# Expert work in jobs of 384 and 256 rows, the first of them among the pieces of the last batch's router

## The chip, the cores and the metric

The kernel runs on one core of one Trainium2 chip. The metric is the device time of one execution in microseconds (us). A core has five engines that run their own instruction lists in order and wait for each other on semaphores: PE (TensorE, matrix products and transposes), DVE (VectorE), ACT (ScalarE), POOL (GpSimd) and SP (SyncE, which here issues most of the DMAs).

## The reference

Two layers on a batch of 8 sequences of 512 tokens with 256 features, all in float32. Layer 0 is an attention, then a mixture of experts behind a router; layer 1 is a second attention and a product with quantized numbers. The part that the change touches is the mixture. Its input is `cat -> int_W1 -> silu -> int_W2 -> norm`, a row of 256 numbers for each token; each token goes to its two best experts, into a slot of a buffer that holds 80 rows for each expert and batch, and each expert is a two-layer perceptron on its 640 rows:

```
probs = softmax(x @ Wr + br);  topk_p, topk_e = top_k(probs, 2)      # x: (8, 512, 256), 8 experts
pos = position of the token among those of its batch that chose the expert
keep = pos < 80
flat_idx = (e_flat * B + b_idx) * 80 + min(pos, 79)
buf = zeros(8 * 8 * 80, 256).at[flat_idx].add(x_rep * keep)          # (expert, batch, slot)
h = relu(buf[e] @ W1[e] + b1[e])                                     # 640 x 256 @ 256 x 1024
y = h @ W2[e] + b2[e]                                                # 640 x 1024 @ 1024 x 256
out = sum over the two choices of y[flat_idx] * p * keep
```

So the 640 rows of an expert are ordered by batch: rows 0 to 399 are those of batches 0 to 4, and row 384 lies inside batch 4.

## The kernel before

**Layer 0 as a pipeline over the batches.** `iteration(b1, b2, b3)` does three things at once: the token part of batch b1 (`token_stream`), the attention of batch b2 (`unit`), and the router part of batch b3 (`router_stream`). The program runs iteration(0, -, -), (1, 0, -), a hardware loop over (b+1, b, b-1), then (-, 7, 6) and last (-, -, 7), in which the router of batch 7 is alone.

**The order is written by hand.** Each engine has its own version of each stream as a Python generator. A generator yields the slot at which its next piece is due; the dictionary `AT` holds these slots. `interleave` goes through the slots 0 to 63, puts one attention unit at every even slot, and `advance` then runs every stream's pieces that are due, one stream after the other in the order in which they were handed to `started`. What comes out is one fixed instruction list per engine. Negative slots run ahead of the first unit; without an attention unit they run when `interleave` comes to slot 0 on DVE (but for `var1`), and earlier, by explicit calls of `advance`, on PE and ACT.

**The router's chain, in its order.** On DVE: moments of x1 (var1), z (normed x1), h1 (nA times the gathered gain, L1183, which waits for the four gathers of `pw` rows), its sum (L1186), moments (var2), h2 (normed with the root that ACT takes in sd2), h2a and h2b (times and plus rows gathered from `cptm`), later y_in, var3, f1, f2, f3 (the last norm), r_in to `rows` (softmax of 8 logits, the two picks, positions, row numbers), which ends in `sidx` (L1271). On POOL: 4 gathers of `pw`, 4 of `cptm`, the products for the t source (L665, L667), 4 gathers of `ms`, the products for the s source (L676, L678), and at the end 8 scatters of nB's rows into `buf_d` (L715). On PE: four sources turned (L767: x, t, h, s; ACT copies them to `cat`, L1004), 16 products with `wint` (L775), 8 with `wint2` (L787), turns of f (L795), the router's 8 products (L803), and sums that give the positions (L811). A float32 product is recorded as two instructions. On SP: loads of `ids` and `boff`, the store of x1 (L612), the load of xN where there is a b2 (L615), the store of the gates (L618).

**The expert stage.** After the last iteration, behind a barrier and with buffers of its own, `expert_loop` does expert after expert, 640 rows each. SP loads rows, b1, W1 (L1432), W2 and b2 (L1434) of expert k when expert k-2 is through, two sets of buffers, and stores y of expert k-2 (L1421). PE turns the 5 row tiles (L1451), multiplies them by W1 (L1463, two halves of 320 columns for each of 8 groups of hidden units, into four banks of PSUM in turn), turns the next expert's rows, and multiplies by W2 (L1475, 5 tiles of 128 rows, 8 products each). ACT takes the ReLU out of PSUM (L1488) into `hid`, of which there is one buffer; DVE copies the turned rows (L1497, L1498) and adds b2 (L1512).

**Layer 1** (`layer1`) comes behind the expert stage and a barrier; it gathers y rows from `y_d`. It is not touched.

## Time and profile before

| | us |
|---|---|
| timed runs | 2714.54, 2724.48, 2725.84 (median 2724.48) |
| profiled execution | 2714.43, of which 2712.4 are the span |
| set-up and the iterations before (-, 7, 6), to 1523.9 | 1523.9 |
| iteration (-, 7, 6), to 1698.5 | 174.6 |
| last iteration (router of batch 7), to 1796.6 | 98.1 |
| expert stage, to 2105.0 | 308.4 |
| layer 1, to 2712.4 | 607.4 |

Over the span PE was busy 78%, DVE 54%, ACT 38% and POOL 31%, and the mean clock granted to TensorE was 0.843 of full speed. All data moved by DMA came to 128.54 MB, 47 GB/s over the span.

In the rows below times are us from the start of the span. A timeline row has start, duration, engine, line and operation, what it writes and reads, the shape, the count where equal neighbours are merged, and in brackets how long the engine was idle before it and what ended that. "PE" rows are products, "PEld" rows weight loads, which overlap them; "SPq" rows are SP's issues of DMAs. The clock is a share of 2.4 GHz.

### The profile page before, as it was taken

The page shows a single profiled execution, that of the slowest core. Times are in us where ns is not written, and L with a number is a line of the kernel's source. Part 1 is how long each engine was busy: PE and PEld are TensorE (multiplying, and loading weights), DVE is VectorE, ACT ScalarE, POOL GpSimd, SP SyncE. Part 2 cuts the span into 40 slices and gives each one's busy share as a digit, 9 for nine tenths or more (in the row PEclk, how much of TensorE's full clock was granted, in tenths as well). Part 3 has the DMA queues.
Part 4 walks back from the last instruction along what each step waited for, and adds up shares of the span by engine and source line. Part 5 has one row for each costly group of instructions (what it writes and reads, how often), then busy time and mean ns, then how long its engine had stood idle before and what let it go on. Part 6 is the DMA issues. An engine that isn't in the chain of part 4 may idle for free. (4 is left out here: it accounts for less than half of the span.)

```text
span 2712.4 us, 33502 instructions
## 1 busy us (share of the span) xinstructions
PE 2108.4 (78%) x11774; PEld 1338.9 (49%) x11774; DVE 1455.8 (54%) x3626; ACT 1024.5 (38%) x2535; POOL 854.1 (31%) x585
## 2 busy tenths in 40 slices
PE   6437879779778878878778798349999496969697
PEld 5215545445444444545445455237777254535454
DVE  2357687577587587577678545220110245464635
ACT  2015545345445345355345355112222241515142
POOL 0253345245354354354254311310000332232311
PEclk9568979779878878878878888669999787979889
DMA  6100020120110200200200200222221301020200
GB/s 239 41 18 1 1 88 1 34 71 1 46 58 1 76 29 1 81 24 1 81 24 1 71 24 15 72 101 105 101 78 44 111 25 56 12 68 0 80 0 16
DMA packets 62592, 128.54 MB, mean 47 GB/s; under 512 B 14564, under 2 KB 39258, under 8 KB 60130
## 3 DMA queue, kind: packets, MB, share of 16 engines
q1 hardware_dynamic: 46570, 76.19, 8.1%
q0 software_dynamic: 15872, 50.35, 6.3%
q8 instruction: 95, 1.56, 0.2%
q14 instruction: 55, 0.45, 0.1%
HBM read 97.04 MB, written 29.46 MB: 47 GB/s over the span
## 5 line engine op out<-in xcount | busy, mean ns | idle before, releaser
L1039 ACT ACTIVATE att_buf<-att_buf,nmin 128x384 f32<-128x384 f32 (+3 forms) x512 | 287.4, 561 | 500.5 <-DVE nmin L1355 500.2
L879 PE MATMUL bank<-kk,qT 32*128 32x512 f32 (+2 forms) x1024 | 321.3, 651 | 86.1 <-DVE nmin L1355 85.4
L706 POOL TENSOR_TENSOR big<-ex_at,kx 128x2048 f32<-128x2048 f32 x64 | 236.0, 3711 | 202.9 <-DVE xt_na L1149 131.9
L906 PE MATMUL bank<-ident,att_buf 128*128 128x128 f32 x1280 | 230.2, 317 | 15.9 <-ACT att_buf L1047 15.0
L652 POOL TENSOR_TENSOR big<-kx 128x1280 f32<-128x1280 f32 x64 | 163.3, 2570 | 211.7 <-ACT kx L978 149.3
L920 PE MATMUL bank<-att_buf,vp 128*32 128x128 f32 x2560 | 218.6, 308 | 0.0
L1047 ACT COPY att_buf<-bank 128x384 f32<-128x384 f32 (+3 forms) x512 | 208.6, 408 | 17.9 <-PE bank L920 16.8
L1344 DVE TENSOR_TENSOR att_buf<-bank,wdiag 128x128 f32<-128x128 f32 x384 | 92.9, 283 | 181.8 <-PE bank L884 180.5
L879 PEld LDWEIGHTS bank<-kk,qT 32*128 32x128 f32 x1024 | 109.4, 213 | 160.0 <-DVE nmin L1355 108.3
L906 PEld LDWEIGHTS bank<-ident,att_buf 128*128 128x128 f32 x1280 | 170.3, 165 | 27.2 <-ACT att_buf L1039 21.7
L715 POOL DMA_INDIRECT buf_d<-nB,sidx x64 | 62.6, 977 | 323.4 <-DVE sidx L1271 306.3
L920 PEld LDWEIGHTS bank<-att_buf,vp 128*32 128x32 f32 x2560 | 135.7, 121 | 56.9 <-issue 46.9
L1488 ACT ACTIVATE hid<-bank,eb 128x320 f32<-128x320 f32 x128 | 67.5, 527 | 240.2 <-PE bank L1463 240.2
L1149 DVE TENSOR_REDUCE xt_na<-big 128x64 f32<-128x1024 f32 x128 | 151.8, 1209 | 11.0 <-POOL big L706 10.2
L1705 POOL TENSOR_SCALAR kf<-kf 128x512 f32<-128x512 f32 x40 | 67.4, 1684 | 256.1 <-ACT kf L1870 255.2
L1463 PE MATMUL bank<-eb,ew 128*128 128x320 f32 x512 | 141.3, 437 | 1.7 <-DVE eb L1498 1.7
L1475 PE MATMUL bank<-ew,hid 128*128 128x256 f32 x640 | 139.6, 379 | 0.6 <-ACT hid L1488 0.6
L1355 DVE CUSTOM_DVE_ANT_0 att_buf<-bank,att_buf 128x128 f32<-128x128 f32 (+3 forms) x320 | 137.5, 444 | 0.0
L1475 PEld LDWEIGHTS bank<-ew,hid 128*128 128x128 f32 x640 | 121.0, 190 | 17.2 <-ACT hid L1488 1.1
L775 PE MATMUL bank<-cat,wint 128*128 128x512 f32 x256 | 123.3, 618 | 0.7 <-ACT cat L1004 0.7
L1463 PEld LDWEIGHTS bank<-eb,ew 128*128 128x128 f32 x512 | 98.4, 192 | 42.6 <-DVE eb L1498 2.1
L824 PE MATMUL bank<-wvl,cT 128*128 128x448 f32 (+1 forms) x256 | 76.3, 464 | 49.0 <-issue 40.6
(342 smaller groups left out, 3970.1 us busy)
## 6 DMA issues: line engine op xcount, KB each, us to landing
ew<-in_eW SPq DMA_DIRECT2D x16, 1024.0 KB, 8.0
buf_d<-zero SPq DMA_DIRECT2D x8, 640.0 KB, 7.8
er<-buf_d SPq DMA_DIRECT2D x8, 640.0 KB, 4.3
y_d<-yy SPq DMA_DIRECT2D x8, 640.0 KB, 9.2
xt_na<-in_xT SPq DMA_DIRECT2D x8, 512.0 KB, 3.5
nA<-in_xN SPq DMA_DIRECT2D x8, 512.0 KB, 3.5
x_d<-x SPq DMA_DIRECT2D x8, 512.0 KB, 3.6
kf<-x_d SPq DMA_DIRECT2D x8, 512.0 KB, 3.2
```

The source lines that it names most:

```text
L652: pool.tensor_tensor(prod[:, lo:hi], spread(kx[:, t, 0:D], 1, hi - lo), spread(kx[:, t, DH * lo:DH * lo + D], 1, hi - lo, DH), ALU.mult)\
L706: pool.tensor_tensor(pv[:, c * P:(c + 1) * P, :].rearrange("p (h d) o -> p o h d", d=DH), spread(ex[:, t, :, 8 * c:8 * c + 8], 3, DH), spr ...
L775: mm = pe.matmul(bank[SIDE[o]][:], wint[:, order[n], o * P:(o + 1) * P], cat[:, n, :], start=(n == 0), stop=(n == 7))
L879: pe.matmul(bank[u % 2][:, 0:n], qT[r:r + 32, g, i * P:(i + 1) * P], kk[r:r + 32, g, T * i * P:T * i * P + n], start=True, stop=False)
L906: mm = pe.transpose(bank[3 + u % 2][:, j * P:(j + 1) * P], pr[:, u % NPR, j * P:(j + 1) * P], ident[:])
L920: mm = pe.matmul(bank[5][r:r + 32, i * P:(i + 1) * P], vp[:, j, p, DH * c:DH * c + 2 * DH], prT[:, (u + x) % 3, j * P:(j + 1) * P], start= ...
L1039: act.activation(pr[:, u % NPR, 0:n], pr[:, u % NPR, 0:n], ACT.Exp, scale=-1.0, bias=nmin[:, u % 4:u % 4 + 1], accum_out=rsum[:, i, h:h + ...
L1047: act.copy(prT[:, u % 3, 0:n], bank[3 + u % 2][:, 0:n]).then_inc(s("prT_ok"), 1)
L1149: dve.tensor_reduce(nA1[:, t, c * w:(c + 1) * w], pv[:, c * w:(c + 1) * w, :], X, ALU.add).then_inc(s("pv_used"), 1)
L1355: dve.tensor_tensor_reduce(dst if x else tiled(dst), lg[:, 0:n] if x else tiled(lg[:, 0:n]), add, 1.0, LARGE, ALU.add, ALU.min, nmin[:, (u ...
L1463: mm = pe.matmul(bank[n % 4][:, 0:W], ew1[:, k % 2, m, o * P:(o + 1) * P], eb[:, k % 2, m, c * W:(c + 1) * W], start=(m == 0), stop=(m == ...
L1475: mm = pe.matmul(bank[4 + n % 4][:, 0:D], hid[:, m, t * P:(t + 1) * P], ew2[:, k % 2, m, :], start=(m == 0), stop=(m == KH - 1))
```

## The change

- The stage `expert_loop` and its buffers go. The work of an expert is cut into two jobs, one of its rows 0 to 383 and one of its rows 384 to 639: first the eight jobs of 384 rows, for all experts, then the eight of 256 rows. Each expert's weights are so loaded twice.
- The jobs run inside the last iteration, iteration(-, -, 7), as a third stream (`expert_stream`) on PE, ACT and DVE behind `router_stream`, with slots of its own. Jobs 0, 1 and 2 have theirs among the router's slots; from job 3 on (on PE from the W2 products of job 2 on) they follow the router's last pieces.
- Buffers lie in layer 0's own: one set in `big` and `ex_at`, one in `kk` and `att_buf`, the hidden units and y in `kk`. Products with W1 use two banks of PSUM instead of four, those with W2 two instead of four.
- Job 0's rows and weights are loaded in the iteration before, (-, 7, 6), once its `ss_ok` has come, ahead of xN. Those of job k from 2 on are issued when job k-2's W2 products are done. SP waits for `e_sent`, which POOL sets when the scatters of batch 7 have landed, ahead of job 8's loads (the first of 256 rows).
- PE turns the rows of job k+1 between the W1 and W2 products of job k, ahead of the wait for job k's last ReLU (before it was behind that wait).

The slots, as `yield` in the streams have them:

```
PE : -4 turned(0) first(0) turned(1) | 2 second(0) | 10 first(1) turned(2) | 28 second(1; tile 0)
     33 second(1; 1, 2) first(2; 0, 1) | 43 first(2; 2) | 47 first(2; 3..7) turned(3) | 55 second(2), job 3, 4, ...
ACT: -4 relu(0) | 11 relu(1) | 38 relu(2; 0, 1) | 43 relu(2; 2) | 50 relu(2; 3..7), job 3, ...
DVE: -4 rows_in(0) | 7 rows_in(1) | 10 rows_out(0) | 12 rows_in(2) | 30, 40, 43 rows_out(1; 0, 1, 2)
     53 rows_in(3) | 62 rows_out(2), rows_in(4), rows_out(3), ...
```

The core of the diff:

```diff
+                JOBS = [(e, lo, hi) for lo, hi in ((0, 3), (3, ST)) for e in range(E)]
+                JT = [hi - lo for _, lo, hi in JOBS]
+                tiles_upto = lambda k: sum(JT[0:k])
...
+                                    for k in range(1, len(JOBS)):
+                                        n = k % 2
+                                        if k >= 2:
+
+                                            sp.wait_ge(s("e_y_mm"), tiles_upto(k - 1))
+                                        if k == E:
+                                            sp.wait_ge(s("e_sent"), 1)
+                                        for dst, src in expert_first(*JOBS[k], n):
+                                            sp.dma_start(dst, src).then_inc(s(f"e_w1_in{n}"), 16)
+                                        if k >= 2:
+                                            sp.wait_ge(s("e_y_ok"), tiles_upto(k - 1))
+                                        for dst, src in expert_second(JOBS[k][0], n):
+                                            sp.dma_start(dst, src).then_inc(s(f"e_w2_in{n}"), 16)
+                                        if k >= 2:
+                                            store(k - 2)
+                                        if k == 4:
+                                            sp.wait_ge(s("sidx_ok"), 1)
+                                            sp.dma_start(gate_d[b3], gi[:].rearrange("p k t -> p (k t)")).then_inc(s("out3"), 16)
...
+                                if b1 is None and b2 is not None:
+                                    for dst, src in expert_first(*JOBS[0], 0) + expert_second(JOBS[0][0], 0):
+                                        sp.dma_start(dst, src).then_inc(s("e_pre"), 16)
                                 if b2 is not None:
                                     sp.dma_start(xN[:], a["xN"][b2]).then_inc(s("xn_in"), 16)
...
+                                if experts:
+                                    pool.memset(ln[:, 0, 0:1], 0.0).then_inc(s("e_sent"), 1)
...
+                                    def turned(k):
+                                        if k:
+                                            pe.wait_ge(s(f"e_w1_in{k % 2}"), 48 * ((k + 1) // 2))
+                                            pe.wait_ge(s("e_rT_ok"), K2 * k)
+                                        for m in range(K2):
+                                            for t in range(JT[k]):
+                                                mm = pe.transpose(bank[m][:, t * P:(t + 1) * P], er[k % 2][:, t, m * P:(m + 1) * P], ident[:])
+                                        mm.then_inc(s("e_rT_mm"), 1)
+
+                                    def first(k, *os):
+                                        n = JT[k] * P
+                                        for o in os:
+                                            if o == 0:
+                                                pe.wait_ge(s("e_rT_ok"), K2 * (k + 1))
+                                            if KH * k + o >= 2:
+                                                pe.wait_ge(s("e_h_ok"), KH * k + o - 1)
...
+                                    def second(k, *ts):
+                                        for t in ts:
+                                            n = tiles_upto(k) + t
+                                            if t == 0:
+                                                if k:
+                                                    pe.wait_ge(s(f"e_w2_in{k % 2}"), 32 * ((k + 1) // 2))
+                                                pe.wait_ge(s("e_h_ok"), KH * (k + 1))
+                                            if n >= 2:
+                                                pe.wait_ge(s("e_y_ok"), n - 1)
...
+                                    for k in range(3, len(JOBS)):
+                                        first(k, *range(KH))
+                                        if k + 1 < len(JOBS):
+                                            turned(k + 1)
+                                        second(k, *range(JT[k]))
...
+                                            if o == 0 and k:
+                                                act.wait_ge(s(f"e_w1_in{k % 2}"), 48 * ((k + 1) // 2))
+                                                act.wait_ge(s("e_y_mm"), tiles_upto(k))
...
+                                side = started(*[g() for g, on in ((router_stream, b3), (token_stream, b1)) if on is not None])
+                                if experts:
+                                    side += started(expert_stream())
...
-        if "B" in parts:
-            expert_loop()
```

## Rows read from the trace of the kernel before

**Rows 1.** Windows by stage: us, busy (instructions) by engine, clock, DMA share, GB/s.

```profile
1698.50:1796.60 98.10, 32.91 (x114) 20.82 (x114) 27.92 (x88) 13.28 (x20) 30.57 (x24) 0.61 0.19 59
1796.60:2105.00 308.40, 290.14 (x1232) 228.69 (x1232) 29.94 (x64) 67.47 (x128) 0.02 (x1) 0.98 0.25 93
```

**Rows 2.** Timeline of the last iteration: start, us, engine, line, what.

```profile
1709.45 1.22 DVE L1183 TENSOR_TENSOR nB<-nA,gac 128x1024 f32<-128x1024 f32 x1 [7.14 <-DMA gac<-in_pw,ids]
1710.71 1.22 DVE L1186 TENSOR_TENSOR nB<-nB,gac 128x1024 f32<-128x1024 f32 x1
...
1720.13 3.20 POOL L667 TENSOR_TENSOR gb<-gb 128x1024 f32<-128x1024 f32 x1
...
1734.49 2.34 POOL L678 TENSOR_TENSOR gac<-gac 128x1024 f32<-128x1024 f32 x1
...
1739.52 15.98 PE L775 MATMUL bank<-cat,wint 128*128 128x512 f32 x32 [0.67 <-ACT cat L1004]
...
1760.11 1.29 DVE L1210 TENSOR_TENSOR nB<-bank,rows 128x512 f32<-128x512 f32 x2 [38.98 <-PE bank L787]
...
1767.80 1.97 PE L795 MATMUL bank<-ident,nB 128*128 128x128 f32 x8 [7.79 <-DVE nB L1186]
...
1770.44 3.58 PE L803 MATMUL bank<-wr,gb 128*128 128x8 f32 x16 [0.67 <-ACT gb L1030]
...
1783.15 0.17 DVE L1271 CAST sidx<-sx 128x8 int32<-128x8 f32 x1
```

**Rows 3.** Timeline of the handover to the expert stage.

```profile
1805.92 1.29 DVE L1497 COPY eb<-bank 128x512 f32<-128x512 f32 x2 [22.60 <-PE bank L1451]
...
1807.60 19.56 PE L1463 MATMUL bank<-eb,ew 128*128 128x320 f32 x64 [1.71 <-DVE eb L1498]
```

**Rows 4.** Timeline of the expert stage: one steady period, and the last addition.

```profile
1827.78 1.31 PE L1451 MATMUL bank<-ident,er 128*128 128x128 f32 x10 [0.62 <-ACT hid L1488]
...
1828.93 17.43 PE L1475 MATMUL bank<-ew,hid 128*128 128x256 f32 x80
...
1846.20 17.39 PE L1463 MATMUL bank<-eb,ew 128*128 128x320 f32 x64
1846.40 0.42 DVE L1512 TENSOR_TENSOR yy<-bank,eb 128x256 f32<-128x256 f32 x1 [3.03 <-PE bank L1475]
1846.85 0.38 SPq L1432 DMA_DIRECT2D er<-buf_d  x1
...
1847.57 0.53 ACT L1488 ACTIVATE hid<-bank,eb 128x320 f32<-128x320 f32 x1 [19.84 <-PE bank L1463]
1847.84 0.43 SPq L1432 DMA_DIRECT2D ew<-in_eW  x1
...
1864.21 1.31 PE L1451 MATMUL bank<-ident,er 128*128 128x128 f32 x10 [0.62 <-ACT hid L1488]
...
2100.33 0.42 DVE L1512 TENSOR_TENSOR yy<-bank,eb 128x256 f32<-128x256 f32 x1 [3.03 <-PE bank L1475]
```

**Rows 5.** Groups by shape over the span: ACT's copies of two widths.

```profile
L1047 ACT COPY att_buf<-bank 128x384 f32<-128x384 f32 x128 | 58.9, 460 | 1.3 <-PE bank L920 1.3
L1047 ACT COPY att_buf<-bank 128x256 f32<-128x256 f32 x128 | 45.5, 356 | 1.9 <-PE bank L920 0.9
```

**Rows 6.** DMA issues, us to landing: W1, W2 issued at 1847.8, 1848.3; at 1800.1.

```profile
ew<-in_eW SPq DMA_DIRECT2D x1, 1024.0 KB, 6.2
...
ew<-in_eW SPq DMA_DIRECT2D x1, 1024.0 KB, 8.2
...
ew<-in_eW SPq DMA_DIRECT2D x1, 1024.0 KB, 13.6
```

**Rows 7.** Windows in the wint products and in the expert stage's first loads.

```profile
1740.00:1744.00 4.00, 4.00 (x6) 1.56 (x6) 0.00 (x0) 0.77 (x1) 0.00 (x0) 0.56 0.00 0
1744.00:1748.00 4.00, 4.00 (x10) 1.71 (x9) 0.00 (x0) 0.00 (x0) 0.00 (x0) 1.00 0.00 0
1799.00:1802.00 3.00, 0.00 (x0) 0.00 (x0) 0.00 (x0) 0.00 (x0) 0.00 (x0) 0.50 1.09 412
```

**Rows 8.** DMA issues over the span, us to landing: the gathers of pw rows.

```profile
gac<-in_pw,ids POOLq DMA_INDIRECT x32, 3.6
```

More of the change, by code:

```diff
@@ L581, in iteration @@
                         s = Sems(lctx, "a")
+                        experts = b1 is None and b2 is None
                         def started(*streams):
@@ L612, in _, with expert_loads, store @@
                                     sp.dma_start(x1_d[b3], x1[:]).then_inc(s("x1_out"), 16)
+                                def expert_loads():
+                                    def store(k):
+                                        e, lo, hi = JOBS[k]
+                                        sp.wait_ge(s("e_y_ok"), tiles_upto(k + 1))
+                                        sp.dma_start(y_e[e][:, lo:hi], yy[k % 2][:, 0:hi - lo]).then_inc(s(f"e_out{k % 2}"), 16)
+                                    for k in range(1, len(JOBS)):
[15 more added lines that the diff above has]
+                                            sp.dma_start(gate_d[b3], gi[:].rearrange("p k t -> p (k t)")).then_inc(s("out3"), 16)
+                                    for k in range(len(JOBS) - 2, len(JOBS)):
+                                        store(k)
+                                    for n in range(2):
+                                        sp.wait_ge(s(f"e_out{n}"), 8 * len(JOBS))
@@ L615, in _ @@
                                     sp.dma_start(xN[:], a["xN"][b2]).then_inc(s("xn_in"), 16)
-                                if b3 is not None:
+                                if b3 is not None and not experts:
                                     sp.wait_ge(s("sidx_ok"), 1)
@@ L620, in _ @@
                                     sp.wait_ge(s("x1_ok"), 1)
+                                if b1 is None and b2 is not None:
+                                    sp.wait_ge(s("e_pre"), 80)
                                 if b3 is not None:
@@ L813, in router_stream, with expert_stream @@
                                     mm.then_inc(s("pos_mm"), 1)
+                                def expert_stream():
+                                    def turned(k):
[13 more added lines that the diff above has]
+                                                pe.wait_ge(s("e_h_ok"), KH * k + o - 1)
+                                            for m in range(K2):
+                                                mm = pe.matmul(bank[2 + o % 2][:, 0:n], ew1[k % 2][:, m, o * P:(o + 1) * P],
+                                                               eb[k % 2][:, m, 0:n], start=(m == 0), stop=(m == K2 - 1))
+                                            mm.then_inc(s("e_h_mm"), 1)
+                                    def second(k, *ts):
[7 more added lines that the diff above has]
+                                                pe.wait_ge(s("e_y_ok"), n - 1)
+                                            for m in range(KH):
+                                                mm = pe.matmul(bank[4 + n % 2][:, 0:D], hid[:, m, t * P:(t + 1) * P], ew2[k % 2][:, m, :],
+                                                               start=(m == 0), stop=(m == KH - 1))
+                                            mm.then_inc(s("e_y_mm"), 1)
+                                    yield -4
+                                    turned(0)
+                                    first(0, *range(KH))
+                                    turned(1)
+                                    yield 2
+                                    second(0, 0, 1, 2)
+                                    yield 10
+                                    first(1, *range(KH))
+                                    turned(2)
+                                    yield 28
+                                    second(1, 0)
+                                    yield 33
+                                    second(1, 1, 2)
+                                    first(2, 0, 1)
+                                    yield 43
+                                    first(2, 2)
+                                    yield 47
+                                    first(2, *range(3, KH))
+                                    turned(3)
+                                    yield 55
+                                    second(2, 0, 1, 2)
+                                    for k in range(3, len(JOBS)):
[3 more added lines that the diff above has]
+                                        second(k, *range(JT[k]))
@@ L1068, in _ @@
                                 side = started(*[g() for g, on in ((router_stream, b3), (token_stream, b1)) if on is not None])
+                                if experts:
+                                    side += started(expert_stream())
                                 advance(side, AT["x"])
```

183 lines of the change are left out of this document (81 added, 102 removed).

## The prediction, made before the changed kernel ran

> **What bounds the kernel now.** The span and its windows by stage [rows 1] come first. The last iteration, which has only batch 7's router left, lasts 98.1 us with PE busy in 32.9; the expert stage behind it lasts 308.4 us with PE busy in 290.1 at a granted clock of 0.98. So one stage is a chain of short steps between engines with TensorE idle, and the next is TensorE's alone. Work that can be carried from the second into the holes of the first is the whole prize: at most 98.1 - 32.9 = 65 us of holes, and the handover between the stages.
>
> The second view is the timeline of the last iteration [rows 2]. DVE's first affine step waits 7.14 us for the gathered rows; POOL's two products end at 1723.3 and let PE turn them; the s source is ready at 1736.8; then the 8 products with wint (15.98 us), the second matrix, a norm, the router's product, and a tail of DVE steps to sidx at 1783.3. The third is the handover [rows 3]: eight scatters, a barrier, the loads, the turns, DVE's copies, and PE's first expert product at 1807.60, 24.3 us after sidx. The fourth is one expert in its steady state [rows 4]: from one turn to the next 36.43 us, of which 17.39 are products with W1 (64 instructions, 0.27 each), 17.43 products with W2 (80, 0.218 each) and the rest ten turns (about 0.115 each) and a 0.62 wait for the last ReLU. It is TensorE's pace, and ACT and DVE idle most of it.
>
> **The change part by part.** I give times from the start of the last iteration (1698.5). The old kernel's last expert product is through when DVE takes it up at 2100.33 [rows 4], so at +401.8.
>
> *Job sizes.* Columns streamed per expert stay the same. By W1 at 0.27 us for 320 columns (0.084 us per hundred) an instruction with 384 takes 0.322 and one with 256 takes 0.216, which is what W2's 256 columns take [rows 4]. A job of 384: 32 x 0.322 = 10.3, six turns 0.7, 48 x 0.2165 = 10.4, and the wait for the last ReLU. A ReLU of 320 columns takes 0.527, and copies of 384 and 256 columns differ by 0.104 [rows 5], so 0.58 and 0.47. It starts about 0.29 after PE could go on (1847.57 against 1846.20 + 4 x 0.27) [rows 4], hence ready after 0.92 and 0.81, of which the turns now cover 0.7 and 0.46: gaps 0.2 and 0.35. Sum 21.6 us for 384 rows and 6.9 + 0.5 + 6.9 + 0.35 = 14.6 for 256, together 36.2 against 36.43: nothing lost. ReLU now has two banks instead of four: with 256 columns it is through 0.81 after, against 0.86 that PE needs for the other bank. I cost that at zero with 0.05 us to spare; if the cover fails, at 0.1 for each of 64 steps, 6 us.
>
> *Weights twice.* 2.1 MB more for each expert, 17 MB in all. In steady state W1 lands 6.2 us after its issue [rows 6], behind 640 KB of rows. PE's last result reaches DVE 0.2 after PE has gone on (1846.40 against 1846.20) and SP's issue of rows comes as soon, 0.25 taken; W1 is issued 0.99 later [rows 4] and so lands at 7.4; with 256 KB of rows instead of 640 it is 0.9 sooner at 412 GB/s [rows 7], 6.5. PE asks for it after one W1 pass of 256 rows, at 6.9. So zero, with up to 0.5 x 7 = 4 us; I take 1. The queue itself has room: 2.5 MB per job at 412 GB/s is 6 us of 14.6.
>
> *Job 0's loads* go onto SP's queue in the iteration before, behind ss_ok and ahead of xN. What they push back is xN, by the 6 us of their transfer; its consumers are POOL's sum with bout, behind which POOL has nothing to do until sidx, and DVE's last addition of that iteration. Zero; I see no row that would make it more than those 6 us.
>
> *The start.* In program order DVE does z and h1 before it copies job 0's turned rows out, and h1 waits for the gathers: h1 ends at +12.2 [rows 2]. Job 1's loads (2.5 MB) now run beside those gathers, behind ids, boff and x1 on SP's queue. The gathers land 3.6 after their issue [rows 8]. If the loads all went first they would end about 6 us after the 512 KB of x1, near +9.5, and the last 256 KB of rows, which DVE had at +10.95, would be some 2 to 3 us late; if not, 0. I take 2. The Trainium skill (DMA: Bandwidth & Descriptors, Queues, rings and completion order) says that each DMA engine goes round its queue rows packet by packet, so the gathers on POOL's queue would hardly wait behind SP's; by it the time would be up to 2 us lower. No row of before has a long load beside these gathers.
>
> *The walk through the iteration*, PE's order being fixed by the slots. Copies of 384 columns, two, 1.1 (of 512, 1.29 [rows 3]): job 0's W1 starts at +15.3. PE has been idle for over 10 us, and the wint products, after two idle stretches, ran at a granted clock of 0.56 for their first 4 us and 1.00 behind [rows 7], the two levels of 1.2 and 2.4 GHz: 2.0 lost. W1 to +27.6; turns of job 1, 28.3; W2 of job 0, 38.8 (ReLU's gap included). Behind it t and h are turned with ACT's copies between, 41.9 (eight turns 1.0 to 1.1, as ten took 1.31 at full clock [rows 4]). ACT could take the second root only after job 0's ReLUs, at about +28.5, so h is ready at some +34: covered. tt is ready at +24.8 [rows 2]. Job 1's W1 and job 2's turns to 52.9; s is turned and copied, 54.9 (ss ready at +38.3 [rows 2]: covered). The wint products, 15.98 less 2.0 for the warm clock, 68.9. One tile of job 1's W2, 72.4; the second matrix, 75.9; two tiles, 82.9, beneath which DVE does y, moments, norm and affine (1760.1 to 1767.8 before [rows 2], 8 us with an addition of job 1 between: f ready at +84); two ReLU groups of job 2, 85.5; turns of f, one group, the router's product (3.58 at half clock [rows 2], 2.1 taken), 89.9; five groups and job 3's turns, 97.0, beneath which DVE does the picks (5 of the 9.1 us between that product's end and sidx before); pos, 97.3; job 2's W2 to **+107.7**. DVE copies job 3's rows, and its last 4 us of steps give sidx at +102; the scatters that follow hold up only job 8. Three jobs are then done, and no wait in this walk over 1 us is left but the first one and ACT's copies behind the turns.
>
> *The rest.* Jobs 3 to 7, 5 x 21.6 = 108; jobs 8 to 15, 8 x 14.6 = 117; less the last job's missing turns, plus 1 for late W1: +333. **Saved: 401.8 - 333 = 69 us.** The last store is 256 KB instead of 640 KB; under 1 us, left out. Cross-check: PE's work moved is three jobs without gaps, 64 us, the handover from sidx to a warm PE goes (some 24 + 2), and the router's tail, the starting wait and the cold start stay.
>
> The profiled run took 2714.4 (span 2712.4 and 2.0 around it), the three timed ones 2714.5, 2724.5, 2725.8: 2645 by the first, 2655 by the median. The spread is not the change's, and I take the middle, **2651 us**.
>
> **The rivals.**
> - *W1 late in the short jobs.* If it lands like W2 does, 8.2 after issue [rows 6], it comes at 9.4 against 6.9: 2.5 x 7 = 18 us, 2669. For: twice the loads in the same time. Against: 6.2 in steady state, less ahead of it. 0.10.
> - *One job fewer fits.* The slots are written by hand, and DVE and ACT take router steps and job steps in one order, so a late router step can hold a job's ReLU or copy. If that costs a job's 21.6 us in waits: 2673. For: at 84 against 85.5 and 94.9 against 97.0 the margins are small. Against: the walk has them in time. 0.12.
> - *It doesn't do what it says*: only job 0 gets in, the two others serialise with the router's steps. 43 us, 2694. For: before, each router step had an idle engine waiting. Against: in PE's order a piece of a job stands between nearly every two router steps, and each has its inputs by the walk. 0.05.
> - *Slower*: the doubled weight traffic sets the pace. W1 of expert 1 landed after 13.6 when 5.6 MB were under way [rows 6]. Landing L us after issue costs each of 7 short jobs L + 1.24 - 6.9 and 2.0 for the cold restart, and each of 5 long ones L + 1.24 - 10.3 and 2.0. That is 69 us at L = 10.8, the point from which the gain is gone; at 13.6 it is 102 us: 2753. Against: 6 us of transfer in a job of 14.6, and 412 GB/s seen. 0.04; 0.03 for ending within 0.5%.
> - *Forecast*, 2637 to 2662: 0.66.
>
> **How the numbers follow.** The low end: 2645 less the 2 for gathers, the 1 for W1 and 4 for seams that I rounded up: 2638. The high end: 2655 + 4 for W1 + the job that doesn't fit: 2681. Faster by over 0.5% (13.6 us, about what a measurement of this kernel tells from no change) is all but the last cases: 0.93; within it 0.03; slower 0.04.
>
> **What would show it.** The last L1512-like addition about 333 us after the last iteration's start; PE's first W1 product of job 0 at +15 behind DVE's h1; PE's clock at 1.00 from about +20 on; job 3's first product at +108; periods of 21.6 and 14.6; PE waiting for W1's DMA under 0.5 us in the short jobs; sidx near +102 instead of +84.8 with nobody late for it. The prediction is wrong if the period of a short job is over 16 us, or if PE waits for ACT or DVE by over 10 us in sum between +20 and +108.

## The result and the profile after

| | before | changed |
|---|---|---|
| timed runs, median | 2725.16 (2714.54 to 2731.16, 4 runs) | 2650.89 (2649.61 to 2665.87, 4 runs) |
| ratio, with its 95% interval | | 0.9737 [0.9703, 0.9771] |
| profiled execution, of which the span | 2714.43, 2712.4 | 2649.61, 2647.8 |
| start of the last iteration | 1698.5 | 1705.7 |
| from there to the last addition of b2 | 401.8 | 337.1 |
| layer 1, from its first load | 607.4 | 600.8 |

The change is faster by 2.6%, 62 to 81 us. The stretch that it touches, from the last iteration's start to the last expert's addition, is 64.7 us shorter in the profiled execution. I call it the **stretch** from here on, since it can be compared without the rest. The medians lie 74.3 us apart; the interval holds both numbers, and the 64.7 is what the runs tie to the change.

First the windows by stage, which answer to [rows 1]: iteration (-, 7, 6), the last iteration up to PE's first product of job 3, jobs 3 to 15, layer 1 (window, us, busy time and instructions by engine, clock, DMA share, GB/s).

```profile
core 0: us, PE busy (x) PEld busy (x) DVE busy (x) ACT busy (x) POOL busy (x), PEclk, DMA share, GB/s
1527.62:1705.67 178.05, 153.06 (x926) 92.62 (x926) 91.67 (x323) 88.33 (x249) 33.33 (x31) 0.84 0.16 51
1705.67:1816.52 110.85, 93.11 (x378) 65.94 (x379) 32.76 (x104) 26.61 (x44) 26.71 (x21) 0.89 0.38 125
1816.52:2046.98 230.46, 223.88 (x969) 176.25 (x967) 23.74 (x56) 53.59 (x104) 3.66 (x6) 1.00 0.45 155
2046.98:2647.80 600.82, 455.58 (x2624) 265.41 (x2624) 288.63 (x532) 199.46 (x328) 170.79 (x137) 0.88 0.13 41
```

The iteration that had PE busy in 32.9 of 98.1 us has it busy in 93.1 of 110.9. The 17.7 us that are left are nearly all at its start, as the timeline shows, which answers to [rows 2, 3]. L697 is a gather, L1341 is h1's multiplication, L1437 the copies of turned rows, L900 the products with W1, L889 turns, L914 products with W2, L834 turns of the router's sources, L842 wint.

```profile
1709.12 0.97 POOL L697 DMA_INDIRECT gac<-in_pw,ids  x1 [6.33 <-DMA boff<-in_boff]
...
1722.40 1.22 DVE L1341 TENSOR_TENSOR nB<-nA,gac 128x1024 f32<-128x1024 f32 x1 [12.89 <-DMA gb<-in_cptm,ids]
1723.54 1.01 DVE L1437 COPY att_buf<-bank 128x384 f32<-128x384 f32 x2
...
1724.61 13.29 PE L900 MATMUL bank<-att_buf,big 128*128 128x384 f32 x32 [16.13 <-DVE att_buf L1437]
...
1749.04 1.04 PE L834 MATMUL bank<-ident,gb 128*128 128x128 f32 x8
1750.89 1.06 PE L834 MATMUL bank<-ident,nB 128*128 128x128 f32 x8 [0.82 <-ACT cat L1136]
1751.80 10.49 PE L900 MATMUL bank<-att_buf,kk 128*128 128x384 f32 x32
1762.12 0.82 PE L889 MATMUL bank<-ident,ex_at 128*128 128x128 f32 x6
1762.77 1.04 PE L834 MATMUL bank<-ident,gac 128*128 128x128 f32 x8
1764.54 14.00 PE L842 MATMUL bank<-cat,wint 128*128 128x512 f32 x32 [0.73 <-ACT cat L1136]
...
1806.08 10.61 PE L914 MATMUL bank<-big,kk 128*128 128x256 f32 x48
1816.52 10.48 PE L900 MATMUL bank<-att_buf,kk 128*128 128x384 f32 x32
```

After 1724.6 PE waits no longer than the 0.82 and 0.73 us behind ACT's copies. Before that it stands still for 16.13 us: its job is ready, its turned rows lie in PSUM, and DVE, which has to copy them out, waits 12.89 us for the gathers of h1. (Its row names a gather of `cptm` rows, because both sets of gathers signal on the same four semaphores; what h1 waits for is the last of the `pw` rows, whose gather was issued at 1712.92 and landed some 9.4 us later.)

The third view has the W1 products of two long jobs in a row, the first and the last of eight W2 passes of short jobs, a wait for weights, and the last addition, which answers to [rows 4].

```profile
1838.16 10.48 PE L900 MATMUL bank<-att_buf,big 128*128 128x384 f32 x32
...
1859.80 10.48 PE L900 MATMUL bank<-att_buf,kk 128*128 128x384 f32 x32
...
1932.45 7.15 PE L914 MATMUL bank<-big,kk 128*128 128x256 f32 x32 [0.17 <-issue]
...
2005.70 0.66 PE L889 MATMUL bank<-ident,ex_at 128*128 128x128 f32 x4 [0.29 <-DMA big<-in_eW]
...
2035.56 7.15 PE L914 MATMUL bank<-kk 128*128 128x256 f32 x32 [0.61 <-issue]
...
2042.74 0.42 DVE L1448 TENSOR_TENSOR kk<-bank,att_buf 128x256 f32<-128x256 f32 x1 [2.93 <-PE bank L914]
```

The period is 21.64 us for 384 rows and 14.7 for 256 (seven periods from 1932.45 to 2035.56). The view of waits from job 3 on shows who stood between the jobs (us in total, times, longest).

```profile
PEld bank L900 <- ACT kk L1175: 1.5, 8, 0.2
...
PEld bank L889 <- DMA big<-in_eW: 1.0, 2, 0.7
...
PE bank L889 <- DMA big<-in_eW: 0.3, 1, 0.3
```

TensorE's products waited 0.3 us for rows and W1 in thirteen jobs (its weight loads, which go ahead of them, 1.2 us, 0.2 of it in a row not shown), and its weight loads waited 1.5 us for ReLUs that had two banks instead of four.

### The profile page after: what moved, and what is told of

Same layout as the page of the kernel before. It is cut to its first block and busy times, and to the rows that moved or that the text cites. A ratio compares the mean times of both kernels' runs of the same rounds, so it can differ in the third digit from the quotient of the medians.

```text
span 2647.8 us, 33574 instructions
## 1 busy us (share of the span) xinstructions
PE 2096.1 (79%) x11774; PEld 1320.3 (50%) x11774; DVE 1440.8 (54%) x3634; ACT 1025.5 (39%) x2535; POOL 852.6 (32%) x586
## 5 line engine op out<-in xcount | busy, mean ns | idle before, releaser
L1036 PEld LDWEIGHTS bank<-ident,att_buf 128*128 128x128 f32 x1280 | 172.4, 167 | 24.5 <-ACT att_buf L1195 18.0
L1175 ACT ACTIVATE kk<-bank,big 128x384 f32<-128x384 f32 (+1 forms) x128 | 67.5, 528 | 215.9 <-PE bank L900 202.4
L842 PE MATMUL bank<-cat,wint 128*128 128x512 f32 x256 | 121.4, 610 | 0.7 <-ACT cat L1136 0.7
L1555 DVE CUSTOM_DVE_ANT_1 att_buf<-bank,att_buf 128x512 f32<-128x512 f32 (+2 forms) x192 | 105.2, 548 | 0.1
L1948 ACT ACTIVATE qs<-bank,qscol 32x512 f32<-32x512 f32 x128 | 86.9, 679 | 40.7 <-PE bank L1843 38.9
L1014 PEld LDWEIGHTS bank<-negb,identb 128*128 128x128 bf16 x512 | 30.1, 100 | 139.4 <-issue 133.8
L1001 PE MATMUL bank<-kk,qT 32*128 32x128 f32 x256 | 64.6, 338 | 44.1 <-DVE nmin L1555 22.2
```

The costliest lines, as they stand in the source:

```text
L842: mm = pe.matmul(bank[SIDE[o]][:], wint[:, order[n], o * P:(o + 1) * P], cat[:, n, :], start=(n == 0), stop=(n == 7))
L1036: mm = pe.transpose(bank[3 + u % 2][:, j * P:(j + 1) * P], pr[:, u % NPR, j * P:(j + 1) * P], ident[:])
L1555: dve.tensor_tensor_reduce(dst if x else tiled(dst), lg[:, 0:n] if x else tiled(lg[:, 0:n]), add, 1.0, LARGE, ALU.add, ALU.min, nmin[:, (u ...
L1948: last = act.activation(v["qs"][r:r + 32, i - 2, :], src[r:r + 32, :], fn, bias=qscol[r:r + 32, i - 2:i - 1])
```

## The experiments

Each run's total is given with its ratio to the kernel before on the same chip. The reading goes by the stretch, because the parts that no experiment touches vary more than what is disputed: the last iteration began anywhere from 1698 to 1714 us, iteration (-, 7, 6) took about 174.4 us or 177.4 to 178.9, and layer 1 took 600 to 620. The stretch repeats: two profiled executions of the kernel before gave 401.8 and 402.1, two of the changed one 337.1 and 336.2.

### Repeats: what can be told apart

**The changed kernel again**, no edit.

> The changed kernel itself, once more. Its stage from the last iteration's start to the last addition should repeat at +337 within 1 us, whatever the rest of the program does; the ratio to the kernel before should be 0.974 within 0.003. If the stage itself moves by several us, the differences of a few us that the other runs show in it mean nothing.

2659.08, ratio 0.9746 [0.9708, 0.9784]; stretch 336.2.

**The kernel before again**, no edit.

> The kernel before, once more, for its stages. Theory: the set-up, the iterations up to the last and layer 1 differ between profiles by several us each for no reason in the code; the last iteration and the expert stage repeat. Then the stage from the last iteration's start to the last addition is 401.8 within 1 us, the iteration (-, 7, 6) comes near the 178 that the other kernels showed, and layer 1 lies between 600 and 620. Rival: the iteration takes 174.5 again, which would put 3.5 us of it on the change (its early loads or its program).

2722.99 (one run); stretch 402.1, iteration (-, 7, 6) 174.4, layer 1 607.4. So a difference of 2 us in the stretch means something, and one of 7 us in the total doesn't. Iteration (-, 7, 6) kept its 174.4, as the rival had it, but that doesn't put 3.5 us on the change: of the profiled executions with the early loads seven took 178.0 to 178.9 and one 174.3, and without them it took 177.4 with the sizes alone and 178.8 with job 0's loads in the last iteration (both below).

### Without the interleaving

```diff
-                                    yield -4
+                                    yield 63
                                     turned(0)
                                     first(0, *range(KH))
                                     turned(1)
-                                    yield 2
                                     second(0, 0, 1, 2)
...
```

The other yields of the three expert streams are taken out in the same way: jobs, buffers and early loads are the changed kernel's, but all jobs stand behind the router's last piece.

> All pieces of the expert stream stand behind the router's last piece on PE, ACT and DVE; job sizes, buffers, loads and the missing barrier stay as in the changed kernel. Theory: of the 65 us won, about 45 come from filling the router's holes and 20 from the handover (no barrier, weights there already). Then sidx comes at about +90, the jobs take 289 us behind it, the last addition comes at +382 (changed kernel +337, before +401.8) and the time is near 2696. Rival: the handover is most of the gain and the interleaved pieces only push the router back; then the last addition comes below +350 and the time is under 2665.

2699.47, ratio 0.9904 [0.9877, 0.9932]; stretch 381.7, as the theory has it. Timeline of PE around the first job:

```profile
1735.86 1.97 PE L834 MATMUL bank<-ident,gb 128*128 128x128 f32 x8 [24.98 <-POOL gb L732]
...
1793.13 1.52 PE L889 MATMUL bank<-ident,ex_at 128*128 128x128 f32 x6
1798.07 12.54 PE L900 MATMUL bank<-att_buf,big 128*128 128x384 f32 x32 [3.42 <-DVE att_buf L1426]
```

This splits the gain. The iteration starts at 1709.35, so the first W1 product comes at +88.7, and 293.0 us later the last addition. In the kernel before these are +109.1 [rows 3] and 292.7. Hence 20.4 us come from the end of the stage boundary (barrier, then rows and weights loaded with nothing to do). The boundary itself gave 23.3, since the first W1 product comes 1.2 us behind `sidx` instead of 24.5; 2.9 of it went back, as `sidx` came at +87.6 instead of +84.7. The cutting into jobs costs nothing here, and the interleaving is worth the other 381.7 - 337.1 = 44.6 us. The same numbers close the account of the changed kernel: 18.9 to its first W1 product, the jobs' 293.0, and 25.2 left over. The router's own work on PE between the jobs comes to that within 0.3 us: 2.8 for t and h and 1.8 for s with ACT's copies waited for, 13.8 wint, 3.5 the second matrix, 0.9 for f, 1.7 the router's product, 0.3 the sums, 24.8 together, and 0.7 that job 0's W1 products lost more to the low clock than behind the router (13.29 against 12.54). Nothing more of the interleaved stretch was lost to the seams.

### The sizes alone

The kernel before, its `expert_loop` over sixteen jobs, with four banks and the turns behind the wait for the last ReLU, as they were:

```diff
-                                for k in range(E):
-                                    pe.wait_ge(s("ebT_ok"), 3 * (k + 1))
-                                    for n in range(2 * KH):
+                                for k in range(len(JOBS)):
+                                    W = JT[k] * P
+                                    pe.wait_ge(s("ebT_ok"), K2 * (k + 1))
+                                    for o in range(KH):
...
```

> The kernel before, its expert stage behind the barrier, with the work of the experts cut into the 16 jobs of 384 and 256 rows (W1 products into four banks, the wait for the last ReLU ahead of the turns as before). Theory: job sizes and doubled weights cost next to nothing: a period of 22.3 and 15.0 us where the ReLU's wait is paid twice per expert, the stage 7 us longer than 308.4, the time near 2732 against 2725. Rival: doubled weight loads come late in the short jobs, 2.5 us each and more; then the stage is longer by 20 to 30 us and PE waits for W1's DMA.

2728.85, ratio 0.9999 [0.9973, 1.0024]; stretch 409.1, which is 7.3 longer, the theory's 7. PE in one long job of it:

```profile
1957.58 10.48 PE L1465 MATMUL bank<-eb,ew 128*128 128x384 f32 x32
1968.73 0.87 PE L1453 MATMUL bank<-ident,er 128*128 128x128 f32 x6 [0.67 <-ACT hid L1491]
1969.44 10.53 PE L1477 MATMUL bank<-ew,hid 128*128 128x256 f32 x48
1979.80 5.65 PE L1465 MATMUL bank<-eb,ew 128*128 128x384 f32 x17
```

22.22 us from W1 to W1 against 21.64. The 0.67 in brackets is the wait for the last ReLU, 0.56 in a short job, paid sixteen times instead of eight. In the changed kernel the turns stand ahead of that wait and cover it: 0.58 us less for each of eight long jobs and some 0.3 for each of eight short ones (15.03 against 14.7) come to 7.0 of the 7.3. That small reordering, which looks like tidying, is what made the job sizes free. The rival didn't occur: beside the first load, TensorE waited for W1 once, 0.76 us. The total alone would have called this edit no change.

### W2 and b2 ahead of rows, b1 and W1 on SP's queue

```diff
-                                        for dst, src in expert_first(*JOBS[k], n):
-                                            sp.dma_start(dst, src).then_inc(s(f"e_w1_in{n}"), 16)
                                         if k >= 2:
                                             sp.wait_ge(s("e_y_ok"), tiles_upto(k - 1))
                                         for dst, src in expert_second(JOBS[k][0], n):
                                             sp.dma_start(dst, src).then_inc(s(f"e_w2_in{n}"), 16)
+                                        for dst, src in expert_first(*JOBS[k], n):
+                                            sp.dma_start(dst, src).then_inc(s(f"e_w1_in{n}"), 16)
```

W1 is issued behind W2 and lands later, which is the prediction's rival of late weights made real. The edit moves the loads of job 1 too, not only those from job 2 on; that cost little, as job 3's first product came at +111.7 instead of +110.9.

> From job 2 on SP issues W2 and b2 ahead of the rows, b1 and W1, so that W1 is issued 1.4 us later and has 1.4 MB ahead of it instead of 0.26. Theory: W1 then lands about 10.1 us after PE has begun the W1 pass of the job before, and PE asks for it after 6.9 in a short job and 10.3 in a long one: 3.2 us of waiting in each of 7 short jobs and nearly none in the long ones, the last addition at +359, the time 22 us longer, with PE's waits for W1's DMA in the short jobs alone. Rival: the loads have slack, or the short jobs wait by more than their cover and cool PE down as well: +340, or +375 and more.

2702.15, ratio 0.9905 [0.9863, 0.9947]; stretch 381.7, 44.6 longer: more than the theory's price for lateness alone, and on the side of the rival, that the waits cool TensorE too. PE in a long job and in two short ones, and windows over the end of a short job's wait and behind it:

```profile
1826.54 0.87 PE L889 MATMUL bank<-ident,ex_at 128*128 128x128 f32 x6 [1.51 <-DMA big<-in_eW]
1827.25 10.53 PE L914 MATMUL bank<-kk 128*128 128x256 f32 x48
...
1979.45 0.66 PE L889 MATMUL bank<-ident,att_buf 128*128 128x128 f32 x4 [3.82 <-DMA kk<-in_eW]
1979.94 8.76 PE L914 MATMUL bank<-big,kk 128*128 128x256 f32 x32
1988.54 7.12 PE L900 MATMUL bank<-att_buf,kk 128*128 128x256 f32 x32
1999.35 0.66 PE L889 MATMUL bank<-ident,ex_at 128*128 128x128 f32 x4 [3.69 <-DMA big<-in_eW]
```

```profile
1979.30:1981.90 2.60, 2.45 (x9) 2.10 (x10) 0.76 (x2) 0.00 (x0) 0.00 (x0) 0.63 0.04 14
1981.90:1983.90 2.00, 2.00 (x7) 1.59 (x7) 0.00 (x0) 0.00 (x0) 0.00 (x0) 0.62 0.00 0
1983.90:1990.00 6.10, 6.10 (x30) 5.38 (x29) 0.85 (x2) 0.32 (x1) 0.00 (x0) 1.00 0.01 3
```

The wait of 3.82 is followed by products at a granted clock of 0.62, between the levels of 1.2 and 2.4 GHz in its mean, and the W2 pass takes 8.76 instead of 7.15. So such a wait costs its own length and 1.6 us more, and a short job takes 19.9 us. All waits for W1 come to 33.2 us, 28.0 of them in the seven short jobs (3.6 to 5.1 each), where the theory had 22, and 5.2 in five long jobs (0.7 to 1.5 each), where it had nearly none; the slower products behind the seven long waits account for most of the rest. The order rows, W1, W2 is what keeps the doubled weight traffic hidden. That the changed kernel waits for W1 at all, if by under 1 us, shows that it has little margin.

### Why job 0 started late

In the changed kernel the gathers of `pw` land 9.4 us after their issue, against 3.6 [rows 8]. Share of the 16 DMA engines by queue (packets, MB, share), of the changed kernel from +6 to +8, from +8 to +10 and from +14 to +16, last of the kernel before from +6 to +8:

```profile
q1 hardware_dynamic: 113, 0.63, 84.3%
q0 software_dynamic: 10, 0.04, 5.2%
```

```profile
q1 hardware_dynamic: 73, 0.49, 64.6%
q0 software_dynamic: 60, 0.21, 29.0%
```

```profile
q0 software_dynamic: 182, 0.63, 92.5%
q1 hardware_dynamic: 60, 0.09, 11.8%
```

```profile
q0 software_dynamic: 108, 0.33, 59.3%
```

q0 carries POOL's gathers, q1 SP's loads. Beside job 1's loads the gathers get 5.2%, then 29.0%, 28.6% and, as the loads run out, 53.9%; once these end they get 92.5%. In the kernel before they have 59.3% from +6 to +8 and 72.3% behind that.

**Job 1's loads behind h1**:

```diff
                                         n = k % 2
+                                        if k == 1:
+                                            sp.wait_ge(s("h1_ok"), 1)
```

> SP holds job 1's loads (2.5 MB) back until DVE has h1. Theory: those loads, on SP's queue, are what made the gathers of pw rows land after 9.4 us instead of 3.6 and DVE's h1 start at +16.7 instead of +10.95. Then the gathers land after some 3.6 again, job 0's first W1 product starts at +13.3, the last addition at +331.5 and the time is near 2645. Rival: the gathers are late for something else (the x1 store, issue times); then they still land after 9 us and nothing moves, 2651.

2654.81, ratio 0.9729 [0.9667, 0.9791]; stretch 330.7, 6.4 less than the changed kernel's and what the theory expects. The gathers land after 3.7 us again, and DVE's wait for them falls from 12.89 to 7.84. h1 starts at +11.7 instead of +16.7, against +10.95 before, so this shows the cause of 5 of its 5.8 us of lateness.

**Job 0's loads at the start of the last iteration** instead of in the one before, so that they too run beside the gathers (5 MB instead of 2.5):

```diff
+                                    for dst, src in expert_first(*JOBS[0], 0) + expert_second(JOBS[0][0], 0):
+                                        sp.dma_start(dst, src).then_inc(s("e_pre"), 16)
                                     for k in range(1, len(JOBS)):
...
-                                if b1 is None and b2 is not None:
-                                    for dst, src in expert_first(*JOBS[0], 0) + expert_second(JOBS[0][0], 0):
-                                        sp.dma_start(dst, src).then_inc(s("e_pre"), 16)
```

with the waits for `e_pre` on PE, ACT and DVE ahead of job 0.

> Job 0's rows and weights are loaded at the start of the last iteration, ahead of job 1's, instead of in the iteration before. Theory: the gathers of pw rows lose to SP's loads for as long as these run; with 5 MB instead of 2.5 they land 5 to 6 us later still, h1 starts near +22 and the last addition comes near +343. The iteration before keeps its 178 us (three kernels with the early loads had 178.0 to 178.8, one without them 177.4). Rival: gathers and loads share the DMA engines evenly, h1 keeps +16.7, and only the wait for job 0's weights (some +13) counts: +337.

2649.8 (one run); stretch 336.3, no longer than with the early loads, so the rival's times held: h1 doesn't come later. PE and DVE:

```profile
1722.53 1.54 PE L888 MATMUL bank<-ident,ex_at 128*128 128x128 f32 x6 [13.51 <-DMA ex_at<-in_eb]
1723.03 1.23 DVE L1342 TENSOR_TENSOR nB<-nA,gac 128x1024 f32<-128x1024 f32 x1 [12.17 <-DMA gac<-in_pw,ids]
```

Job 0's loads are there when DVE comes out of its wait, at +16.0, so the early loads bring nothing in the changed kernel as it stands. The gathers of `pw` land 8.7 us after issue, not later than with half the loads beside them. The rival's reason, an even share, isn't borne out: from +6 to +8 they moved nothing, from +8 to +10 they had 25.8%. The rest of the loads fell on the gathers of `cptm`, which landed after 10.9 us instead of 5.6, and no wait of TensorE came of that here.

**Job 0's rows copied ahead of h1** on DVE:

```diff
                                 advance(side, AT["var1"])
+                                if experts:
+                                    advance(side[-1:], AT["z"])
```

> DVE copies job 0's turned rows right behind the moments of x1, ahead of z and h1. Theory: the only large hole left in the changed kernel is PE's 16.1 us wait for DVE's copy, which stands behind h1 and so behind the gathers. Then job 0's first W1 product starts near +4.5 us of the last iteration instead of +18.9, every later piece moves up by some 14 us, the last addition comes at +323 instead of +337.1, and the time is near 2637 (2650.9 less 14). Rival: the router's own chain (gathers, t and s sources, norms) is hardly covered and takes over as soon as PE is earlier; then PE waits for tt, ss or f instead, the last addition stays above +330 and the time above 2644.

2655.46, ratio 0.9731 [0.9681, 0.978]; stretch 326.6, 10.5 less, between the theory's 323 and the rival's 330. PE:

```profile
1717.47 12.38 PE L900 MATMUL bank<-att_buf,big 128*128 128x384 f32 x32 [1.11 <-DVE att_buf L1437]
...
1741.30 5.41 PE L914 MATMUL bank<-big,kk 128*128 128x256 f32 x16 [3.60 <-DVE kk L1448]
```

Job 0's W1 starts at +3.8 instead of +18.9, 15.1 sooner. About a third is given back: job 0's third tile of W2 needs a bank that DVE frees by an addition, which stands behind the router's steps in DVE's order. PE waits 3.60 us there and goes on slower, 5.41 us for sixteen products that took 3.62 in the changed kernel; the W1 products at the start lost 0.9 less than there (12.38 for 13.29).

**Both, and the addition sooner**: rows first, the first addition at slot 5, and job 1's W2 and b2 (not its W1) behind `h1_ok`:

```diff
                                             sp.dma_start(dst, src).then_inc(s(f"e_w1_in{n}"), 16)
+                                        if k == 1:
+                                            sp.wait_ge(s("h1_ok"), 1)
...
+                                    yield 5
+                                    rows_out(0, 0)
                                     yield 7
                                     rows_in(1)
                                     yield 10
-                                    rows_out(0, 0, 1, 2)
+                                    rows_out(0, 1, 2)
...
+                                if experts:
+                                    advance(side[-1:], AT["z"])
```

> Three edits together: DVE copies job 0's turned rows ahead of z and h1; DVE adds b2 to job 0's first tile one place earlier (behind h2, ahead of h2a and the copies of job 1's rows); SP holds job 1's W2 and b2 (1.15 of the 2.5 MB) back until h1 is there. Theory: with the first edit alone the last addition came at +326.6, and PE then waited 3.6 us for DVE's addition; that wait goes and the addition comes at +323, 14 us before the changed kernel's +337.1; the time is 14 us under that of the changed kernel on the same chip, near 0.968 of the kernel before. Rival: the next router step that is late takes it back: +326 or more, no better than the first edit alone.

2645.25, ratio 0.9712 [0.9674, 0.9751]; stretch 326.3: no gain on the version before it, so the rival held. The wait for the addition is gone, and another has come:

```profile
1723.18 10.63 PE L916 MATMUL bank<-big,kk 128*128 128x256 f32 x48
1737.24 1.19 PE L836 MATMUL bank<-ident,gb 128*128 128x128 f32 x8 [3.43 <-POOL gb L734]
...
1740.93 12.47 PE L902 MATMUL bank<-att_buf,kk 128*128 128x384 f32 x32
```

PE is now through job 0 before POOL has made the t source, waits 3.43 us for it and goes on cold: job 1's W1 takes 12.47 instead of 10.49. W2's load had moved onto the gathers of `cptm`, which the t source needs: DVE waited 3.04 and POOL 8.10 us for them. One thing here was not the edit's doing as far as the runs show: job 0's W1 products took 10.59 us, at a granted clock of 1.00 from their start, where the same products took 12.38 in the version before it and 12.22 in the next.

**The same with job 1's W2 behind the t source** (`tt_ok` for `h1_ok`):

```diff
                                         if k == 1:
-                                            sp.wait_ge(s("h1_ok"), 1)
+                                            sp.wait_ge(s("tt_ok"), 1)
```

> As the kernel with three edits, but SP holds job 1's W2 and b2 back until POOL has the t source, so behind the gathers of cptm rows too. Theory: there the last addition did not come before +326.3 because the router took over: PE waited 3.4 us for the t source and ran the next 4 us cold, and that source was late because the cptm gathers ran beside job 1's W2 (DVE waited 3.0, POOL 8.1 us for them). With the load gone from there the t source comes 5 us earlier, PE neither waits nor cools, and the last addition comes at +321. Rival: the ms gathers, now beside the loads of job 1's W2 and of job 2, make the s source late instead, and the addition stays at +325 or later.

2645.73, ratio 0.9738 [0.9704, 0.9773]; stretch 334.3, 8.0 worse than the version before it; here too the rival held. PE:

```profile
1727.91 1.09 PE L836 MATMUL bank<-ident,gb 128*128 128x128 f32 x8 [0.31 <-POOL gb L734]
...
1744.45 1.10 PE L891 MATMUL bank<-ident,ex_at 128*128 128x128 f32 x6 [3.25 <-DMA big<-in_eW]
1749.85 1.97 PE L836 MATMUL bank<-ident,gac 128*128 128x128 f32 x8 [4.29 <-POOL gac L745]
1752.49 17.02 PE L844 MATMUL bank<-cat,wint 128*128 128x512 f32 x32 [0.68 <-ACT cat L1138]
```

The t source is in time, though only 1.5 us earlier than in the version before it (+28.2 for +29.7) where the theory had 5. But the loads of jobs 1 and 2 now come later and closer together, beside the gathers of `ms`: PE waits 3.25 for job 2's weights and 4.29 for the s source, and wint, cold, takes 17.02 instead of 14.00. Of the 8.0 us, 1.6 are job 0's W1 products, which had no such luck with the clock. The gathers of `pw`, `cptm` and `ms` and the loads of jobs 1 and 2 share some 40 us, and moving a load off one gather puts it onto the next.

The two versions with the shortest stretch, 326.6 and 326.3, are 9.6 to 10.8 us better there than the two executions of the changed kernel. Their ratios, 0.9731 and 0.9712, have intervals that overlap its 0.9737 and 0.9746, so as a total this is not shown.

## Why the prediction was right, point by point

**Which stage and which resource.** Right. The time came out of TensorE's holes in the last iteration and out of the boundary behind it, and jobs behind the router without interleaving gave each its size: 44.6 and 20.4 us. The boundary was put at "some 24 + 2": 23.3 from `sidx` on, of which the later `sidx` took 2.9. Neither sign that would have made the prediction wrong showed: a short job takes 14.7, and PE's waits for ACT between +20 and +108 come to 1.55 us (0.82 and 0.73).

**Job periods.** 21.6 and 14.6 predicted, 21.64 and 14.7 measured. The scaling from 320 columns to 384 and 256, and the turns as cover for the last ReLU, held; the sizes alone showed what that cover is worth, 0.6 us in a long job and 0.3 in a short one.

**Job 0's loads.** Zero, and so it was: xN landed 10.6 us after its issue, at 1598.8, and DVE took it up at 1699.5.

**ReLU with two banks.** Zero with a bound of 6; 1.5 us of waits on weight loads, which overlap the products.

**W1 late.** 1 us taken, 0.3 of PE's waiting measured. The two rivals on it did not occur. The price of the first was too low, though: I had 2.5 x 7 = 18 us for late W1 with the wait alone, and the run with W2 first shows 1.6 us of cold clock on top of a wait of 3.8. The second had 2.0 us of cold clock for each wait, where that run shows 1.6 behind 3.8 and none behind waits of up to 1.5.

**The gathers of h1.** Here the term was mis-sized: "I take 2", between 0 and 3; the landing went from 3.6 to 9.4, and DVE's step from +10.95 to +16.7, 5.8 late. I took the loads to go first and to end at +9.5. They did go first, but were not through at +9.5: from +8 to +14 q1 still held 45 to 73% of the engines. The Trainium skill (DMA: Bandwidth & Descriptors, Queues, rings and completion order), cited for a cost near 0, says that a DMA engine goes round its queue rows a packet at a time. I had read that as an even share, and the trace does not bear that out: 113 packets against 10 in the two microseconds from +6, while gathers were waiting. The turns themselves it doesn't show. Through the late gathers the first W1 product came at +18.9 for +15.3.

**The cold clock.** 2.0 taken, 2.8 measured (13.29 against 10.48 for the same products). Together with the late start that made 4.6 us at the first product with W2 of job 0 (+32.9 for +28.3).

**The walk.** From there on it gained 1.4 in sum, no step being off by more than a microsecond or so: t at +43.4 (38.8), wint at +58.9 (54.9), f at +89.1 (85.5), job 2's W2 at +100.4 (97.3), job 3 at +110.9 (107.7), last addition at +337.1 (333). None of the close margins that carried the rival of one job fewer failed; sidx came at +105 for +102, and nobody waited for it.

**The sum.** 69 us saved by the steps, 64.7 measured. The last addition is 4.1 later than forecast: 4.6 by the two terms above, 1.4 gained in the walk, 0.9 lost in the jobs behind it (226.2 for 225.3). That the median lies at 2650.9 beside a forecast of 2651.0 is partly luck: I had taken the middle between two baselines 10 us apart, and in the profiled execution the last iteration began 7.2 us later and layer 1 was 6.6 shorter, which cancel. Neither belongs to the change as far as the runs show: a kernel with the early loads also took 174.3 for iteration (-, 7, 6), and one without them 177.4. In layer 1 each of four like parts took one of several lengths with a clock to match: its second part 143.4 us at 0.88 in the kernel before and 150.1 at 0.84 in its repeat, the same code on the same data. What decides it is open.

## What to carry to other kernels

When two streams are merged by hand, add up what the bound engine does and then read the first wait of the merged stretch. Here the seams cost nothing and the one wait at the start was 16 us long, of which moving one copy won back 10, because the copy that releases TensorE stood behind another stream's gather. Place bulk loads by what else moves in that stretch, and try their order within a queue by the consumer that comes first: the same bytes in another order were worth 45 us. Judge an edit of a few microseconds by the stretch it touches and show with a repeat that this stretch holds still, since the total of a program this long does not.

## What the runs showed of the hardware

- POOL's gathers first hardly move beside loads on SP's queue and then get a quarter or so: 5.2% of the DMA engines from +6 to +8 in the changed kernel and 29% in each of the next two windows of 2 us, against 59.3% and 72.3% in the kernel before. With job 0's rows first it was 2.4% from +2.3 to +9.3, the first gather being issued at +4.0.
- It is no fixed precedence either: with the loads doubled the gathers of `pw` landed after 8.7 us, not later than the 9.4 with half of them, and had 25.8% and 38.2% of the engines from +8 to +12 while SP's loads were still under way. How the engines choose is left open.
- Waits of 3.4 to 5.1 us on TensorE were followed by slower products: 8.76 for 7.15 behind 3.82 (granted clock 0.62), 12.47 for 10.49 behind 3.43 (0.61 in the first 4 us, 0.53 in the next), 5.41 for 3.62 behind 3.60 (0.57), and 17.02 for 14.00 behind two waits, 3.25 and 4.29, less than 6 us apart (0.50 in the first 8 us). Behind waits of up to 1.5 us the products kept their time: 10.53 behind 1.51, at a granted clock of 1.00.
